# Query build of the first round moved into the loop, and the epilogue of every head pair one step later

## What is computed

```python
c_kv = h @ W_dkv + b_dkv                      # 1024 -> 128
c_q  = h @ W_dq + b_dq
k, v = c_kv @ W_uk + b_uk, c_kv @ W_uv + b_uv # 16 heads of 48 and of 64
q    = c_q @ W_uq + b_uq
q_rot, k_rot = rotary(c_q @ W_qr + b_qr), rotary(h @ W_kr + b_kr)
scores = einsum('bqhd,bkhd->bhqk', [q, q_rot], [k, k_rot]) / 8
out = einsum('bhqk,bkhd->bqhd', softmax(scores), v)
x = layernorm(h + out @ W_o + b_o)
y = layernorm(x + x @ int4(W_ffn) + bias + (x @ a) @ b)
```

## Time and profile before

| | us |
|---|---|
| runs of the kernel before: median of 3 (lowest, highest) | 3230.98 (3227.2, 3246.75) |
| the profiled execution | 3223.21 |
| its span, slowest core (core 1) | 3221.7 |
| spans of the eight cores | 3194.4 to 3221.7 |
| mean granted clock of TensorE, by core | 0.874 to 0.884 |
| busy on core 1: TensorE matmuls / ScalarE / VectorE / GpSimd | 2518.3 / 2195.0 / 1154.3 / 231.9 |
| first exponential of the loop on core 1 | 451.69 |

### The profile page before, as it was taken

How to read it: one execution, slowest core, us unless ns; L and a number is a source line. 1 busy time by engine, 2 the same in 40 slices (tenths; PEclk the granted TensorE clock), 3 DMA queues, 4 the chain that set the end, 5 groups by cost and what they waited for, 6 DMA issues and landing times.

```text
span 3221.7 us, 40178 instructions; the slowest of 8 cores (3194.4 to 3221.7 us)
## 1 busy us (share of the span) xinstructions
PE 2518.3 (78%) x10584; PEld 792.2 (25%) x10584; DVE 1154.3 (36%) x1482; ACT 2195.0 (68%) x2481; POOL 231.9 (7%) x393
## 2 busy tenths in 40 slices
PE   2355759989788888898889888887898888988733
PEld 1122312222222222222222222222222222222211
DVE  1375112213443243323432434144323442343244
ACT  1133349989677977887679866986788677977600
POOL 4000000000000000000000000000000000010000
PEclk8566679999899999999989988998899899999866
DMA  6322230001212121202120122012111211121121
GB/s 111 107 88 90 71 77 22 22 14 39 84 37 71 34 66 60 69 27 71 54 73 28 55 65 76 29 42 83 44 60 42 69 55 55 37 76 55 51 92 39
DMA packets 89939, 188.44 MB, mean 58 GB/s; under 512 B 20579, under 2 KB 50532, under 8 KB 89476
## 3 DMA queue, kind: packets, MB, share of 16 engines
q1 hardware_dynamic: 44292, 82.81, 8.8%
q0 software_dynamic: 31616, 77.88, 8.5%
q10 hardware_dynamic: 13824, 25.17, 2.1%
HBM read 144.65 MB, written 51.64 MB: 61 GB/s over the span
## 4 chain that ended last, share of the span: by engine, by line
PE 52%; DVE 14%; DMA 11%; ACT 10%; issue 10%; POOL 2%; DVEq 0%; SPq 0%; ACTq 0%; POOLq 0%
PE PS L237 50%; ACT Psb L249 5%; DVE bcast_sb L280 3%; DMA bcast_sb<-rden 3%; DVE tA L254 3%; ACT bcast_sb L249 2%; PE PS L243 2%; DMA rden<-bcast_sb 2%; ACT wkr_sb L249 2%; DVE h L254 1%; DMA h<-h 1%; DVE Qsb L260 1%; DMA x_scr<-tA 1%; DVE Psb L260 1%; POOL Vsb L284 1%
## 5 line engine op out<-in xcount | busy, mean ns | idle before, releaser
L249 ACT ACTIVATE Psb<-PS 128x1024 bf16<-128x1024 f32 x1536 | 1522.4, 1041 | 396.4 <-PE PS L237 378.8
L237 PE MATMUL PS<-Psb,Vsb 128*65 128x512 bf16 x3072 | 998.4, 408 | 109.9 <-ACT bcast_sb L249 106.4
L237 PE MATMUL PS<-Qsb,Ksb 64*128 64x512 bf16 x4096 | 831.9, 399 | 103.5 <-ACT Psb L249 63.9
L249 ACT ACTIVATE wkr_sb<-PS 128x1024 bf16<-128x1024 f32 x512 | 534.3, 1044 | 93.1 <-PE PS L237 92.7
L237 PEld LDWEIGHTS PS<-Qsb,Ksb 64*128 64x128 bf16 x4096 | 222.2, 93 | 968.2 <-issue 966.1
L237 PEld LDWEIGHTS PS<-Psb,Vsb 128*65 128x65 bf16 x3072 | 220.4, 112 | 483.9 <-issue 483.9
L237 PE MATMUL PS<-wkr_sb,Vsb 128*65 128x512 bf16 x1024 | 332.5, 408 | 2.6 <-ACT wkr_sb L249 2.6
L280 DVE RECIPROCAL bcast_sb<-bcast_sb 128x512 f32<-128x512 f32 x64 | 214.5, 3352 | 280.2 <-DMA bcast_sb<-rden 280.0
L276 DVE CAST oun_sb<-PS 64x512 bf16<-64x512 f32 x128 | 87.4, 683 | 550.2 <-PE PS L237 547.5
L254 DVE TENSOR_TENSOR tA<-PS,h 128x512 f32<-128x512 f32 x128 | 88.4, 690 | 507.2 <-PE PS L237 466.1
L237 PE MATMUL PS<-wbuf,osb 128*128 128x512 bf16 x512 | 171.2, 422 | 80.0 <-DVE tA L254 63.6
(11 more groups left out here) (88 smaller groups left out, 1378.7 us busy)
## 6 DMA issues: line engine op xcount, KB each, us to landing
h<-h SPq DMA_DIRECT2D x64, 512.0 KB, 3.9
wbuf<-wo_p POOLq DMA_DIRECT2D x32, 512.0 KB, 6.2
bcast_sb<-rden POOLq DMA_DIRECT2D x128, 128.0 KB, 3.0
x_scr<-tA POOLq DMA_DIRECT2D x32, 512.0 KB, 3.0
wbuf<-wf_p POOLq DMA_DIRECT2D x32, 512.0 KB, 5.6
h<-x_scr SPq DMA_DIRECT2D x32, 512.0 KB, 3.8
out<-tA ACTq DMA_DIRECT2D x32, 512.0 KB, 2.7
o_dram<-oun_sb ACTq DMA_DIRECT2D x64, 128.0 KB, 1.7
```

What stands on the lines that cost most here:

```text
L237: e.matmul(o, l, r, start=s1, stop=s2, tile_position=t, skip_group_check=k)),
L249: e.activation(o, i, f, scale=sc, bias=b)),
```

## The change

The Q build of round 0 is advanced ahead of the loop only until pair 0 is built; the same generator, with pairs 1 to 7 left in it, then is the first entry of the loop's list of Q builds, so that it gives one pair per step from kc 3 of pair 0 on. Two variables that nothing reads are dropped. In the epilogue's chain each place is one step later: 2, 4, 7 and 12 instead of 1, 3, 6 and 11.

```diff
-    for _ in qbuild_gen(0, list(range(NP)), True):
-        pass
+    _g0q = qbuild_gen(0, list(range(NP)), True)
+    while (0, 0) not in qb_ready:
+        next(_g0q)
...
-    bg_qb = []
+    bg_qb = [_g0q]
...
-        qR_needed = qb_state["done_qR"]
-        qb_dv = qb_state["done_dv"]
...
-            while gctr[0] < ph(1):
+            while gctr[0] < ph(2):
                 yield "spin"
             wdma0 = dma("gpsimd", rden[PIDX2:PIDX2 + 1, 0:512], bcast_sb[0:1, 0:512],
...
-            while gctr[0] < ph(3):
+            while gctr[0] < ph(4):
                 yield "spin"
             bl = dma("gpsimd", bcast_sb[0:64, :],
...
-            while gctr[0] < ph(6):
+            while gctr[0] < ph(7):
                 yield "spin"
             rr = recip(bcast_sb[:, :], bcast_sb[:, :],
...
-            while gctr[0] < ph(11):
+            while gctr[0] < ph(12):
                 yield "spin"
             od = dma("scalar", o_dram[PIDX2 * 128:(PIDX2 + 1) * 128, :],
```

## The result

The changed kernel takes 3182.7 us, the kernel before 3226.6 us on the same chip (medians of ten runs each); the ratio is 0.9861, interval 0.9838 to 0.9884, so 45 us or 1.4% less. The forecast was 3193.9 us, 37.1 us less. The profiled execution takes 3185.9 us, with a span of 3184.3 us on its slowest core, core 7. A core's span differs from its neighbour's by up to 27 us, so the rest compares means over all eight cores: 3206.8 us before, 3170.3 after, 36.5 less.

A forecast was written before the change was run, and what follows sets the result against it. Bound: ScalarE's free step of 0.91 us, plus single waits tied to the kc 1 copies. Terms -2.4 - 15.5 - 6.4 - 6.4 - 6.4 = -37.1 us from 3231.0 gave 3193.9 us; own range -55 to -25, range given 3170 to 3228.

The forecast's parts named there:

- Part 1: Q build of round 0: first exponential 6.3 us earlier, seven matmuls moved into pair 0 cost 3.9; -2.4 us.
- (a): Transfer at kc 12 in 17 quiet pairs (full clock, late product): next exponential no longer waits; -15.5 us, least gain 12.9.
- (b): Pair 2, rounds 1 to 7: ScalarE's wait for stv at kc 15 shorter by 0.92 each; -6.4 us.
- The rule: Epilogue waits ending at a time fixed by the kc 1 copies shrink by min(wait, 0.92 us) per step moved.
- (c): Pair 3: waits at kc 13 and 27 shrink 0.92 each, Qsb wait at kc 24 gives 0.92 back; -6.4 us.
- (d): Pairs 4 and 5: VectorE's own chain sets the reciprocal and moves along; 0, or -5.5 if data bounded it.
- (e): Pair 6: TensorE's wait behind the reciprocal shrinks 0.92 in seven rounds; -6.4 us, between 0 and -10.
- A: Waits re-form in pairs 2, 3 and 6, leaving only Q build and transfer gains: -17.9, 3213.1 us; chance 0.23.
- B: Shift does nothing, since VectorE reaches the reciprocal itself a step later: -2.4, 3228.6 us; chance 0.08.
- C: Clock falls behind the start of all 31 other pairs too: +7.2 us, 3238.2 us; chance 0.05.
- D: Later transfer makes its reader a step late in each of 64 pairs: +59 less 37.1, 3252.9 us; chance 0.02.

The follow-up runs named there:

- e3: Kernel before with only the o_dram transfer one step later, tail released at the old place: 3205.4 us, ratio 0.9963.
- e4: Kernel before with only the tail one step later (norm_ set later), transfer and other epilogue places unchanged: 3207.2 us, ratio 0.9956.
- e7: Changed kernel with all four epilogue places one further step later (3, 5, 8, 13): 3157.7 us, ratio 0.9780 to the kernel before.
- e10: Changed kernel with all four epilogue places two further steps later (4, 6, 9, 14): 3120.2 us, ratio 0.9677 to the kernel before.
- e2: Kernel before with all four epilogue places one step later, Q build of round 0 as before: 3187.7 us, ratio 0.9904.
- e5: Kernel before with the next tail's first loads held until the latest epilogue's product is done: 3214.1 us, ratio 0.9981.
- e8: Changed kernel with the transfer of the normalised output issued by SP instead of ScalarE: 3282.3 us, ratio 1.0193 to the kernel before.
- e12: Changed kernel with all four epilogue places three further steps later (5, 7, 10, 15): 3134.6 us, ratio 0.9710 to the kernel before.
- e6: Changed kernel with the next tail's first loads held until the latest product is done: 3184.1 us, ratio 0.9897 to the kernel before.
- e9: Against e7, the transfer issued by SP, one step behind the tail's output load: 3163.6 us, ratio 0.9805 to the kernel before.

## Why the prediction was right, and where its terms were off

**What bounds it** held. ScalarE's free step and waits tied to the copies at kc 1 are what the change moved against each other; the reciprocals of the quiet pairs start where they did (on the mean 8.37 us behind the copies before, 8.28 after).

**Part 1** (forecast -2.4): -6.6 to the first exponential and +2.7 in pair 0, -3.9. The first term is right (forecast -6.3). The second was put at 3.9: at full clock TensorE's steps with a wq_sb matmul took 1.38 us, near the 1.45 I had assumed, but the two at half clock cost 0.3 us together instead of 1.2, since those steps are slow in the kernel before as well (1.59 and 1.35 us).

**(a)** (forecast -15.5): the excess in the quiet pairs fell by 16.3 us, by 15.0 in e3. Right. What is left is 12.2 us over 28 quiet pairs; the forecast's lower price, 12.9 with the transfer's own cost on top, was too careful.

**(b)** (forecast -6.4): pairs 1 and 2 together gave -9.3, of which 7 x 0.80 = 5.6 is the transfer of pair 1; 3.7 is left. The rule held: the wait behind stv ends 18.4 us behind the exponential of kc 2 before and 18.2 after, one step further on. What failed is the step that a shorter wait costs nothing behind it. The clock fell behind this wait in 26 of 56 cases before and in all 56 after; the five steps behind it take 6.0 us without a fall and 7.7 with one, so (56 - 26)/8 x 1.7 = 6.4 us per core were given back. With the tail alone (e4), where the clock did not fall more often behind this wait, pair 2 gives -8.3 us against the 6.4 of the forecast. In e7 it fell in 7 of 56 and in e10 in none, and that is part of their gain: of its loop TensorE spends 338 us at half clock before, 304 after, 277 in e7 and 245 in e10 (means of eight cores). I had counted falls at the pairs' boundaries alone. Why the fall comes always after the change and in half of the cases before, I can't say: the wait is shorter (mean 2.39 us over a free step against 2.81), with 1.59 us in e4 it still falls in 24 of 56, and with 3.50 in e3 in 46. The transfer's new place goes with it (e2: 54 of 56); by what way is not shown.

**(c)** (forecast -6.4): -7.1. The giving back at the Q build is there (0.82 us in the step of kc 24), and the last wait gives 1.43, more than a step. The first gives less than a step: its own step is 1.00 shorter, but it ends 18.8 us behind the exponential of kc 2 instead of 18.2. The reciprocal itself starts at +9.24 instead of +8.69 us there: VectorE's chain had only 1.64 us to spare and now has 0.38. So the size is right, but two of its parts miss in opposite directions.

**(d)** (forecast 0): -0.3 and +1.6. Right.

**(e)** (forecast -6.4, 0 to -10): -16.6, the term that was mis-sized. It holds two things. The data land 1.28 us earlier (e4 and e5 show that the tail's loads did it: -8.5 us when they alone are moved), which I had named as a possibility and priced at no more than 3.6. And the step that now goes ahead of the wait isn't a free one of 0.92 us but one with tail matmuls (1.49 us at kc 8 after). To that I put the other 8.1 us, 1.16 per round, as what is left; no run shows it by itself.

**The sum.** Forecast -37.1; the terms measured are -3.9 - 16.3 - 3.7 - 7.1 + 1.3 - 16.6 = -46.3. Of (a), 5.2 us were lost again in other steps of the same pairs: their entries in the table are -4.7, +1.5, -5.6 and -2.3, together -11.1. That makes -41.1. In the profiled execution the phase ahead of the Q build, which the change does not touch, was 4.8 us longer, and with that the spans' mean fell by 36.5. The medians' 45 has an interval of 37 to 52, and -41 lies in it. So the sum is near by luck in part: (b) was 2.7 us short, (a) lost 5.2 again and pair 5's side was 1.3 off, while (e) gave 10.2 more than forecast and part 1 another 1.5. The forecast's own bounds add up to -52, not -55, and -55 to -25 from 3231 is 3176 to 3206, not 3178 to 3208; the measured time is inside either. Whether those 5.2 us are chance of the clock or a cost of the shift, I leave open.

**The rivals.** A came true in one place, pair 2, though not as a longer wait but as a fall of the clock. B fell: the reciprocals of the quiet pairs and of pair 2 stayed, and pair 6's came 0.9 us earlier. In pairs 3, 4 and 5 they did come later (by 0.55, 0.60 and 1.56 us, means of 56), where VectorE's own chain sets them. C did not occur: 29.6 falls at boundaries per core before, 28.1 after. D did not occur in the change; it is what e8 and e12 made, through SP's order: a later place costs nothing until a reader stands behind it.

**What I missed** is the size of what lies further on. The epilogue was moved by one step; moving it by three gives 105 us, and I had twice forecast (e7, e10) that the gain would be used up.

## What to carry to other kernels

When background work is spread over a steady loop, look for each wait at what fixes its end. A wait fixed by a DMA chain begun earlier shrinks by the length of each step that is put ahead of it, so try several shifts, not one, and stop where a load falls behind another stream's work in its queue. Look at what else is on the DMA engines while the critical transfer flies, and count the falls of the clock behind every wait that you change.

## What the hardware showed that was not expected

- The granted clock can fall to 0.50 behind a TensorE pause of 1.97 us, and hold at 1.00 behind one of 2.33; in pair 2 it went from 26 falls in 56 to 56 in 56 while the pause became shorter.
- Loads of 128 KB and one of 512 KB on SP, in flight beside POOL's two broadcasts, delay these by 1.2 to 1.3 us on the mean of 56 cases.
- In the profiled execution of e6 the granted clock was 0.81 for 132 to 566 us of each core's loop, in e9's and e7's on some cores only, and in the other eleven profiled executions nowhere in the loop.
- A transfer that waits in SP's queue costs as much as one that waits in ScalarE's, or more, if a load that TensorE needs stands behind it: 3.05 us of wait at one place, 64 us over the program.
